# Low parts of a recurrent state from a scan, matmul tiles over interleaved places, and work of a block in halves

## The reference

```python
def step(h, xs):
    xzt, xrt, xht = xs                       # seq @ W_z, seq @ W_r, seq @ W of this step
    z = jax.nn.sigmoid(xzt + h @ U_z + vz)
    r = jax.nn.sigmoid(xrt + h @ U_r + vr)
    hh = jnp.tanh(xht + r * h @ U + vh)
    h_new = (1.0 - z) * h + z * hh
    return (h_new, h_new)
```

## Time and profile before

| what | value |
|---|---|
| median of the runs | 6800.1 us (3 runs, 6799.94 to 6800.25) |
| profiled execution, its own time | 6811.76 us |
| its span | 6809.9 us |
| mean granted TensorE clock | 0.996 |
| PE busy | 5998.4 us, 88%, 200232 instructions |
| DVE busy | 4955.6 us, 73%, 43503 instructions |
| ACT busy | 3331.6 us, 49%, 22603 instructions |
| DMA queue of the transfers | 5.5% of 16 engines |

### The profile page before, as it was taken

The page is one execution under the profiler, slowest core; times in us unless marked ns, Lnnn a source line. Parts: engine busy times, 40 slices in busy tenths (PEclk is TensorE's granted clock), DMA queues, the critical chain, the costliest instruction groups (busy, mean ns, idle before and its releaser), DMA issues.

```text
span 6809.9 us, 488240 instructions
## 1 busy us (share of the span) xinstructions
PE 5998.4 (88%) x200232; PEld 5642.2 (83%) x200232; DVE 4955.6 (73%) x43503; ACT 3331.6 (49%) x22603; POOL 3.5 (0%) x13
## 2 busy tenths in 40 slices
PE   7888888888888888888888888888888888888888
PEld 7888888888888888888888888888888888888888
DVE  5777777777777777777777777777777777777777
ACT  3444444444444444444444444444444444444444
POOL 0000000000000000000000000000000000000000
PEclk8999999999999999999999999999999999999999
DMA  2000000000000000000000000000000000000000
GB/s 84 17 18 15 18 17 18 17 17 17 18 17 18 15 18 17 18 18 15 18 17 18 17 18 15 18 17 18 17 17 17 18 17 18 15 18 18 17 18 15
DMA packets 80315, 129.97 MB, mean 19 GB/s; under 512 B 12336, under 2 KB 18480, under 8 KB 80304
## 3 DMA queue, kind: packets, MB, share of 16 engines
q1 hardware_dynamic: 80304, 129.81, 5.5%
HBM read 20.46 MB, written 8.65 MB: 4 GB/s over the span
## 4 chain that ended last, share of the span: by engine, by line
PE 71%; DVE 26%; issue 3%; SPq 0%; DMA 0%; ACT 0%; ACTq 0%; DVEq 0%
PE pair_r L252 30%; PE ps_z L252 24%; PE pair_h L252 17%; DVE pair_h L487 8%; DVE h_part L522 5%; DVE h_part L541 4%; DVE h_part L527 2%; DVE keep L523 2%; DVE zn L536 2%; DVE h_part L532 2%; PE ps_z L212 0%; DMA u_raw<-in_L_cond_U 0%; PE ps_o L212 0%; DVE u_max L424 0%; PE ps_x L224 0%
## 5 line engine op out<-in xcount | busy, mean ns | idle before, releaser
L252 PEld LDWEIGHTS pair_r<-h_part,u_part 128*128 128x128 f16 x65536 | 1845.1, 96 | 1119.9 <-DVE h_part L541 1115.8
L252 PE MATMUL pair_r<-h_part,u_part 128*128 128x32 f16 x65536 | 2048.7, 177 | 771.1 <-DVE h_part L541 758.6
L252 PE MATMUL pair_h<-rh_part,u_part 128*128 128x32 f16 x65536 | 2016.6, 177 | 12.5 <-DVE rh_part L505 12.5
L252 PE MATMUL ps_z<-h_part,u_part 128*128 128x32 f16 x65536 | 1961.5, 176 | 0.0
L252 PEld LDWEIGHTS pair_h<-rh_part,u_part 128*128 128x128 f16 x65536 | 1842.8, 96 | 17.3 <-DVE rh_part L505 15.7
L252 PEld LDWEIGHTS ps_z<-h_part,u_part 128*128 128x128 f16 x65536 | 1795.3, 95 | 0.0
L487 DVE TENSOR_REDUCE pair_r<-pair_r 128x4 f32<-128x20 f32 x4096 | 759.4, 186 | 818.1 <-PE pair_r L252 615.1
L351 ACT ACTIVATE pair_r<-pair_r 128x4 f32<-128x4 f32 x4096 | 644.8, 158 | 1445.1 <-DVE pair_r L487 1182.4
L487 DVE TENSOR_REDUCE pair_h<-pair_h 128x4 f32<-128x12 f32 x4096 | 717.7, 175 | 665.7 <-PE pair_h L252 665.7
L351 ACT ACTIVATE th_z<-ps_z 128x8 f32<-128x8 f32 x2048 | 364.1, 178 | 1046.0 <-DVE ps_z L487 1046.0
L337 ACT ACTIVATE pair_h<-xp 128x8 f32 (+1 forms) x2049 | 369.9, 181 | 807.8 <-DVE zn L536 807.8
(11 more groups left out here) (70 smaller groups left out, 3275.9 us busy)
## 6 DMA issues: line engine op xcount, KB each, us to landing
w_stage<-w_in SPq DMA_DIRECT2D x384, 256.0 KB, 2.3
x_tok<-in_x SPq DMA_DIRECT2D x68, 128.0 KB, 2.6
out_dram<-o_tok SPq DMA_DIRECT2D x66, 128.0 KB, 2.3
mlp_w<-in_L_cond_W SPq DMA_DIRECT2D x2, 1024.0 KB, 6.9
u_raw<-in_L_cond_U_r SPq DMA_DIRECT2D x1, 1024.0 KB, 5.6
u_raw<-in_L_cond_U_z SPq DMA_DIRECT2D x1, 1024.0 KB, 7.6
u_raw<-in_L_cond_U SPq DMA_DIRECT2D x1, 1024.0 KB, 10.3
w_in<-in_L_cond_W_r SPq DMA_DIRECT2D x4, 256.0 KB, 9.8
```

The source lines that it names most:

```text
L252: last = nc.tensor.matmul(bank[:, SLOT * m:SLOT * m + WIDE].rearrange("p (r n) -> p r n", n=n), u_part[:, g, part, k, gm * P:(gm + 1) * P] ...
```

## The change

- The low part comes from a scan. State, tanh and factor lie interleaved in `r_scan` and `n_scan`, three values for each place (0, tanh, h or z); the parts lie at every third place (`STEP`). The scan takes factor times running value less the data: it forms 1, 1 + tanh (or tanh), the full product less the high part. The f32 products of lines 500 and 536 go; `zn` is made once for both halves, after the parts, with a wait of its own before `h_cur`.
- Tiles stream runs of 8 places (`RUN`), of which two are used. Slots are 40 wide instead of 34, and `total` reads with a stride.
- The tanhs of r and h are written to SBUF instead of PSUM.
- In r, three tiles (six matmuls) of the outputs' second half go ahead of the wait for the state's second half, instead of two; in h it stays two.
- ACT writes r's seed behind h's first tanh instead of behind z's, and PE waits for it (`r_seeded`). h's seed waits for no `zn` any more.
- The work of a block goes in halves over the first four steps, PE's and ACT's output a step later. `hist` is laid out by place, not by step. The projection's store moves to the fifth step of a round, between the sums of z and of h.

```diff
-    WIDE = 32
-    SLOT = WIDE + B
...
+    STEP, RUN, WIDE = 3, 8, 32
+    SLOT = WIDE + RUN
+    PITCH = HS * STEP
...
-        hist = sb("hist", [P, 2 * TB, S])
+        hist = sb("hist", [P, S, 2 * TB])
...
-        h_cur = sb("h_cur", [P, S])
-        h_part = sb("h_part", [P, K, 2 * PARTS, B], F16)
-        rh = sb("rh", [P, S])
-        rh_part = sb("rh_part", [P, K, PARTS, B], F16)
+        r_scan = sb("r_scan", [P, S, STEP])
+        n_scan = sb("n_scan", [P, S, STEP])
+        h_cur, z_mul = r_scan[:, :, STEP - 1], n_scan[:, :, STEP - 1]
+        h_part = sb("h_part", [P, 2 * 2 * PARTS * PITCH + RUN], F16)
+        rh_part = sb("rh_part", [P, 2 * PARTS * PITCH + RUN], F16)
...
         def cols(bank, g, m0, m1):
-            slots = bank[:, SLOT * m0:SLOT * m1].rearrange("p (m c) -> p m c", c=SLOT)
-            return slots[:, :, SLOT - ADDENDS[g] * B:SLOT].rearrange("p m (a b) -> p m a b", b=B)
+            runs = bank[:, SLOT * m0:SLOT * m1].rearrange("p (m a c) -> p m a c", c=RUN, m=m1 - m0)
+            return runs[:, :, SLOT // RUN - ADDENDS[g]:, STEP - 1:STEP * B:STEP]
...
+        def part_of(parts, count, hf, part):
+            at = (hf * count + part) * PITCH
+            return parts[:, at:at + PITCH]
+        def place(parts, count, hf, part, step=STEP - 1):
+            return part_of(parts, count, hf, part).rearrange("p (s c) -> p s c", c=STEP)[:, :, step]
...
+            nc.gpsimd.memset(rh_part[:, :], 0.0).then_inc(s["rh_zero"], 1)
...
+            for hf in range(2):
+                for step in range(STEP - 1):
+                    nc.gpsimd.memset(place(rh_part, PARTS, hf, 0, step), -1.0)
...
-                n = (ADDENDS[g] - 1) * B
-                moving = parts[:, k, :, :].rearrange("p a b -> p (a b)").unsqueeze(1).broadcast_to([P, WIDE // n, n])
+                n = ADDENDS[g] - 1
+                at = k // HC * n * PITCH + k % HC * B * STEP
+                runs = parts[:, at:at + n * PITCH].rearrange("p (a c) -> p a c", c=PITCH)[:, :, 0:RUN]
+                moving = runs.unsqueeze(1).broadcast_to([P, WIDE // (n * RUN), n, RUN])
                 for part in range(PARTS):
-                    last = nc.tensor.matmul(bank[:, SLOT * m:SLOT * m + WIDE].rearrange("p (r n) -> p r n", n=n),
+                    last = nc.tensor.matmul(bank[:, SLOT * m:SLOT * m + WIDE].rearrange("p (r a c) -> p r a c", a=n, c=RUN),
                                             u_part[:, g, part, k, gm * P:(gm + 1) * P], moving,
                                             start=first and part == 0, stop=False, skip_group_check=True)
...
+                def product(mh, m, k):
+                    return tile_product(banks[mh], m, g, mh * HC + m, k, parts, k == 0 and m == 0)
+                first, second = ([(m, k) for m in range(HC) for k in range(kh * HC, (kh + 1) * HC)] for kh in range(2))
+                ahead = 3 if g == R else 2
                 pe.wait_ge(s[src + "0"], t1)
-                for m in range(HC):
-                    product(0, m, 0)
-                product(1, 0, 0)
+                for m, k in first:
+                    product(0, m, k)
+                for m, k in first[:ahead]:
+                    product(1, m, k)
                 pe.wait_ge(s[src + "1"], t1)
-                for m in range(HC):
-                    last = product(0, m, 1)
+                for m, k in second:
+                    last = product(0, m, k)
                 last.then_inc(s[name + "0_mm"], 1)
-                for m in range(1, HC):
-                    product(1, m, 0)
-                for m in range(HC):
-                    last = product(1, m, 1)
+                for m, k in first[ahead:] + second:
+                    last = product(1, m, k)
                 last.then_inc(s[name + "1_mm"], 1)
...
+                    pe.wait_ge(s["r_seeded"], t1)
                     staggered(ps_r, R, h_part, "hs", "r", t1)
...
-                        tanh(ps_r[hf][:, TANH:TANH + HS], ps_r[hf], R, HS, f"r{hf}_sum", t1, f"r{hf}_th")
-                    A(hist[:, prv, :], h_cur[:, :], ACT.Copy)
+                        tanh(r_scan[:, half[hf], 1], ps_r[hf], R, HS, f"r{hf}_sum", t1, f"r{hf}_th")
+                    A(hist[:, :, bass.ds(prv, 1)], h_cur.unsqueeze(2), ACT.Copy)
                     tanh(th_z[:, :], ps_z, Z, S, "z_sum", t1, "z_th")
-                    seed(pair_r, R, nxt)
                     act.wait_ge(s["z_th"], t1)
                     A(z_keep[:, :], th_z[:, :], ACT.Copy, scale=-0.5, bias=0.5).then_inc(s["z_keep"], 1)
-                    A(z_mul[:, :], th_z[:, :], ACT.Copy, scale=H_SCALE / 2, bias=H_SCALE / 2)
-                    tanh(ps_h[0][:, TANH:TANH + HS], ps_h[0], H, HS, "h0_sum", t1, "h0_th")
+                    A(z_mul, th_z[:, :], ACT.Copy, scale=H_SCALE / 2, bias=H_SCALE / 2)
+                    tanh(n_scan[:, half[0], 1], ps_h[0], H, HS, "h0_sum", t1, "h0_th")
+                    seed(pair_r, R, nxt).then_inc(s["r_seeded"], 1)
                     seed(ps_z, Z, nxt)
-                    tanh(ps_h[1][:, TANH:TANH + HS], ps_h[1], H, HS, "h1_sum", t1, "h1_th")
-                    act.wait_ge(s["zn1"], t1)
+                    tanh(n_scan[:, half[1], 1], ps_h[1], H, HS, "h1_sum", t1, "h1_th")
                     seed(pair_h, H, nxt)
-                    if turn is not None and u == 1:
-                        act.wait_ge(s["o_sum"], turn)
...
+                    if turn is not None and u in (1, 2):
+                        act.wait_ge(s["o_sum"], act.snap(turn * 2 + (u - 2)))
+                        A(y_cur[:, half[u - 1], :], y_next[:, half[u - 1], :], ACT.Copy).then_inc(s["y_copied"], 1)
...
-            def step(t1):
-                kc = (slice(0, HC), slice(HC, K))
+            def step(t1, proj):
+                def low(parts, count, hi, hf, factors, done):
+                    V.tensor_tensor_scan(part_of(parts, count, hf, hi + 1), factors[:, half[hf]].rearrange("p s c -> p (s c)"),
+                                         part_of(parts, count, hf, hi), 0.0, ALU.mult, ALU.subtract).then_inc(s[done], 1)
                 def gated_high(hf):
                     dve.wait_ge(s[f"r{hf}_th"], t1)
-                    V.scalar_tensor_tensor(rh_part[:, kc[hf], 0, :], kb(ps_r[hf][:, TANH:TANH + HS]), 1.0,
-                                           kb(h_cur[:, half[hf]]), ALU.add, ALU.mult)
-                def gated_full(hf):
-                    V.scalar_tensor_tensor(rh[:, half[hf]], ps_r[hf][:, TANH:TANH + HS], 1.0, h_cur[:, half[hf]],
-                                           ALU.add, ALU.mult).then_inc(s[f"rh32_{hf}"], 1)
+                    V.scalar_tensor_tensor(place(rh_part, PARTS, hf, 0), r_scan[:, half[hf], 1], 1.0,
+                                           h_cur[:, half[hf]], ALU.add, ALU.mult).then_inc(s[f"rhi{hf}"], 1)
                 def gated_low(hf):
-                    dve.wait_ge(s[f"rh32_{hf}"], t1)
-                    V.tensor_tensor(rh_part[:, kc[hf], 1, :], kb(rh[:, half[hf]]), rh_part[:, kc[hf], 0, :],
-                                    ALU.subtract).then_inc(s[f"rh{hf}"], 1)
+                    dve.wait_ge(s[f"rhi{hf}"], t1)
+                    low(rh_part, PARTS, 0, hf, r_scan, f"rh{hf}")
...
+                if proj is not None:
+                    store_projection(*proj)
                 dve.wait_ge(s["h0_mm"], t1)
...
                     dve.wait_ge(s[f"h{hf}_th"], t1)
-                    V.tensor_tensor(h_part[:, kc[hf], NEW, :], kb(z_mul[:, half[hf]]),
-                                    kb(ps_h[hf][:, TANH:TANH + HS]), ALU.mult)
-                def new_full(hf):
-                    V.tensor_tensor(zn[:, half[hf]], z_mul[:, half[hf]], ps_h[hf][:, TANH:TANH + HS],
-                                    ALU.mult).then_inc(s[f"zn{hf}"], 1)
+                    V.tensor_tensor(place(h_part, 2 * PARTS, hf, NEW), z_mul[:, half[hf]],
+                                    n_scan[:, half[hf], 1], ALU.mult).then_inc(s[f"nhi{hf}"], 1)
                 def new_low(hf):
-                    dve.wait_ge(s[f"zn{hf}"], t1)
-                    V.tensor_tensor(h_part[:, kc[hf], NEW + 1, :], kb(zn[:, half[hf]]), h_part[:, kc[hf], NEW, :],
-                                    ALU.subtract).then_inc(s[f"hs{hf}"], 1)
+                    dve.wait_ge(s[f"nhi{hf}"], t1)
+                    low(h_part, 2 * PARTS, NEW, hf, n_scan, f"hs{hf}")
                 dve.wait_ge(s["h1_mm"], t1)
                 total(ps_h[1], H, HC, "h1_sum")
                 new_high(0)
-                new_full(0)
                 keep_low()
                 new_low(0)
                 new_high(1)
-                new_full(1)
                 new_low(1)
-                V.tensor_tensor(h_cur[:, :], keep[:, :], zn[:, :], ALU.add).then_inc(s["h_ok"], 1)
-            def store_projection(count, i, ring):
-                dve.wait_ge(s["proj_mm"], count)
+                V.tensor_tensor(zn[:, :], z_mul, n_scan[:, :, 1], ALU.mult).then_inc(s["zn_ok"], 1)
```

(58 more changed lines are left out.)

38 lines of the change are left out of this document (18 added, 20 removed).

## The result

| | changed kernel | kernel before, same chip |
|---|---|---|
| median | 6928.98 us (4 runs, 6922.7 to 6930.62) | 6800.18 us (6799.94 to 6800.75) |
| ratio | 1.0186, interval 1.0171 to 1.0201 | |
| profiled execution | 6922.7 us, span 6920.9 | 6811.76 us, span 6809.9 (not one of the four runs above) |
| mean granted clock | 0.965 | 0.996 |

The forecast, 6640 (6560 to 6740), has the wrong sign. The changed kernel's page: the busy times of part 1, then the chain of part 4.

A forecast was written before the change was run, and what follows sets the result against it. Bound: a dependence loop through PE, DVE and ACT, once per step, 2048 times. Step 3.258 to 3.185 gains 150 us, block work 11, together 161; profiled 6811.76 to 6651, median 11.7 lower: 6640, range 6560 to 6740.

The forecast's parts named there:

- r's seed and the waits: Seed moved behind h's first tanh: ACT's 0.02 delay covered by r's 14 matmuls, seed done 0.3 early, so no cost.
- a wait on r's seed shows on PE: Sign, to be looked for in the trace after the change, that the prediction is wrong.
- a cost not seen: An unseen cost on the step's loop that eats the whole gain; chance 0.04.
- h_cur is done near T+0.54, with 0.2 to spare.: On DVE, T being the step's first r matmul: h_cur may grow by 0.2 us before it costs.
- the 3.34: Step time in us, 384 times, read from the earlier trace as projection's store plus the inner loop's turn.
- r's stop: PE's halt in r for the new state's second half, forecast to go, by little, with 14 matmuls ahead of it.
- The store's 2.26 to 2.35: Projection's store ends that many us after the step's first r matmul; h0's sum is due at 2.33.
- Tiles: Rival: separate runs double the matmuls' streaming, 26.7 ns apart instead of 25.3; 241 us more, 6881; chance 0.06.
- scan: Rival: the scan's fixed cost is twice as high, 326 ns, adding 141 ns twice a step; 7217; chance 0.04.
- cheap: Rival: scan takes 171 ns and tanh 158, step 3.155 us; 6579; chance 0.12.
- dearer: Rival: strided sums add 25 ns a step (6691), a scan of 206 besides gives 6777; nearer 6700; chance 0.24.
- The stop stays: Rival: r still halts for the state's second half, plus two more matmuls: 0.03 a step, 6700; within a 0.24 chance.

The follow-up runs named there:

- h_cur late: Kernel before, with the f32 product of both halves made once more behind the last low part and h_cur waiting for it: 7041.41 us, ratio 1.0344.
- all three mended: Changed kernel with PE's two waits ahead of r swapped, first projection weights issued ahead of the output, zn made before the second low part: 6646.06 us, ratio 0.9765.
- the seed in its old place: Changed kernel with r's seed back behind z's tanh, PE's wait on it removed, first projection weights issued ahead of the output: 6748.05 us, ratio 0.9907.
- `zn` early: Changed kernel, r's seed behind z's tanh without PE's wait, first weights ahead of the output, zn made before the second low part: 6652.35 us, ratio 0.9777.

## Why the prediction was wrong

**The step that failed: "r's seed and the waits", costed at nothing.** "The seed is done some 0.3 before PE asks for it" was right, and beside the point. Only one wait stays on the first weight load, the one written first; in the trace the other is an instruction of its own ahead of it (the views above leave such instructions out). Here the seed's wait keeps the weight load, and the state's, which ends last, is that other: it goes at 3403.245 and takes 0.051, the weight load follows at 3403.321, the matmul at 3403.352, where the scan had ended at 3403.20. With the waits swapped the seed's is the one apart, over 0.3 earlier, and the weight load goes on the scan's signal. The quiet step shows 0.073 of some 0.09 (3.273 against 3.200), since r, starting later, runs 0.02 faster (0.95 against 0.97). That it is the wait is shown twice, by the order alone and by the kernel before with the wait added. By ratio it is 0.0173, 118 us. The prediction named "a wait on r's seed shows on PE" as the sign of its being wrong, and gave a cost not seen a chance of 0.04.

**The queue that was not costed.** The halves move the output a step later; the sum counted DVE's and ACT's work and left out the output's transfers and what stands behind them. The slack could have been read: `w_stage` was issued at 3451.85, takes 2.3 to land, and was wanted at 3454.95, some 0.8 to spare against a move of 2.16. PE asks for it 0.6 sooner besides, counted from x_tok, since its steps there are shorter. The first piece of the projection now waits 2.07 for its weights, 32 times; shown by the queue's order, 63 to 69 us.

**"h_cur is done near T+0.54, with 0.2 to spare."** True for a quiet step (3403.64 and 0.17: T + 0.46). At the turn of a loop DVE's own branch and register work stands behind `h_cur`. In the changed kernel's trace the branch begins 0.09 behind the start of `h_cur` and the next sum 0.47 behind that: 0.56, and as much with the waits swapped and with h_cur late, 0.545 with all three mended. The kernel before gives no price: 0.54 passes there at a turn and in any other step alike, since its sum waits for PE. A `h_cur` 0.12 later makes r0's sum 0.14 later. It holds 12 steps of a block, the 11 behind the inner turns and the one behind the outer. The prediction read the turn into the earlier trace rows as part of the 3.34; by the medians that step holds the store alone, and the one behind the turn took 3.258. What that is worth depends on the quiet step beside it: 0.139 a turn over 3.273, 0.213 over 3.200, as DVE sets the turn's step (3.412, 3.413) whatever PE could do. From the seed in its old place to `zn` early the block falls by 2.95, 94 us.

**What held.** The scan took 182 ns (forecast 185, bounds 171 and 206), the sums 186 and 174, r's tanh 176 and h's 168 (174), z's matmuls 0.96, so the tiles cost nothing; high to low is 0.20; r's stop is gone. The groups of the changed kernel, busy us and mean ns:

```profile
L526 DVE TENSOR_TENSOR_SCAN rh_part<-r_scan,rh_part 128x12 f16<-128x12 f32 x4096 | 747.3, 182 | 140.6
...
L563 DVE TENSOR_TENSOR h_part<-n_scan 128x4 f16<-128x4 f32 x4096 | 694.3, 170 | 1.1 <-ACT n_scan L381 0.2
...
L589 DVE SCALAR_TENSOR_TENSOR oT<-hist,y_cur 128x256 f32<-128x256 f32 x66 | 28.0, 425 | 0.8 <-ACT hist L420 0.3
L485 DVE TENSOR_TENSOR y_next<-ps_x,gate 128x256 f32<-128x256 f32 x66 | 27.9, 424 | 1.0 <-PE ps_x L219 0.2
```

The Trainium skill ("DVE: opcode table, instruction layouts, handler registers and perf-mode slots", Datapath and trigger behaviour) has tensor_tensor_scan at half throughput. The prediction's estimate from it, 163 and 21 ns, is 184, with which the trace agrees (182). The Trainium skill ("Advanced Engine Details and Errata", Memory Cachelines) says that a different line of SBUF with every access costs time. For VectorE the trace agrees: hist read in order takes as long as y_next, 425 and 424 for 256 elements, where read at 32-byte steps it took 1085 against 684 for 512.

**Mis-sized.** The quiet step without the fault is 3.200, not 3.185: 31 us, the last low part began 0.01 late (T + 2.96) and its way to PE took 0.06, not 0.052. With all three mended the store between the sums and the turn behind it cost 0.02 together and not 0.08, and steps 1 to 4 0.15 and not 0.32, so 0.92 a block, 30 us the other way. The store's 2.26 to 2.35 doesn't follow at its high end: with the register work behind the sum the same terms give 2.47. In the trace of the changed kernel DVE takes h0's sum at T + 2.34, 0.02 late. The kernel with all three mended has a block of 205.16 against the forecast's 205.12, and 0.9765 of 6800 is 6640. That the two agree so closely is luck, as 31 and 30 us cancel; and the sum was that of a kernel which the change was not.

**Of the rivals** none had this mechanism. "Tiles" and "scan" are refuted (spacing 25.3 ns, scan 182), "cheap" too, and so are the strided sums of "dearer" (186 ns as before). "The stop stays" did not come about. Two tiles ahead brought the stop back without its two added matmuls and cost 0.033 a step, close to the 0.03 of that rival.

**Left open.** 274 of the 289 us are in the medians of the steps, and that is all of what the profiled execution shows: 6922.7 against the 6651 that the sum gave for it, 272. The rest comes from comparing the median with 6640, 11 less, since the profiled execution before lay 11.7 above the median of its runs. No run shows such a difference for the changed kernel, whose profiled execution lies 6 below its median. What brings on the stretches of lower clock, below, was not settled.

## What to carry to other kernels

A wait that is always met is not free where it shares an instruction with the wait that ends last: write the late one first, and look in the trace at which instruction each wait sits on. When work is moved by a step, follow its output through every queue to whatever stands behind it there. And the slack of an engine's last instruction in a loop body is counted to the branch, not to the next sum: measure it at the turn, not in a quiet step.
